# Second cross attention: five of the ten heads that VectorE shifts by their row maximum are shifted on GpSimd

## The reference, cut to what matters

```python
q = layer_norm(query_antecedent @ Wq, gq, bq)
k = layer_norm(key_antecedent @ Wk, gk, bk)
v = layer_norm(value_antecedent @ Wv, gv, bv)
...
sim = jnp.einsum('bhqd,bhkd->bhqk', qh / jnp.sqrt(jnp.float32(dk)), kh)
bias = NEG_BIAS * (~mask).astype(sim.dtype)[:, None]
masked = sim + bias
weights = jax.nn.softmax(masked, axis=-1)
outh = jnp.einsum('bhqk,bhkd->bhqd', weights, vh)
```

## Time and profile before

| what | value |
|---|---|
| median of 3 runs | 1052.25 us |
| lowest and highest of them | 1049.93 and 1054.67 us |
| span of the profiled execution | 1057.6 us |
| busy share of the span: PE, DVE, ACT, POOL | 87%, 74%, 53%, 46% |

### The profile page before, as it was taken

How to read it: one execution, slowest core, us unless ns; L and a number is a source line. 1 busy time by engine, 2 the same in 40 slices (tenths; PEclk the granted TensorE clock), 3 DMA queues, 4 the chain that set the end, 5 groups by cost and what they waited for, 6 DMA issues and landing times.

```text
span 1057.6 us, 19542 instructions
## 1 busy us (share of the span) xinstructions
PE 919.4 (87%) x6337; PEld 655.6 (62%) x6337; DVE 785.7 (74%) x2080; ACT 557.7 (53%) x1494; POOL 490.0 (46%) x451
## 2 busy tenths in 40 slices
PE   6898985888778999869997598988989999989987
PEld 4787533767578989727775243434437677768774
DVE  6889999999756777769998376777734744589982
ACT  4675456886444445724443156766764233445533
POOL 5444553555066564635556777574530600024430
PEclk9999896999879999969999659989999999999998
DMA  9300000000111111410000322222102000000001
GB/s 324 149 1 1 2 6 1 1 1 1 41 39 39 41 40 33 109 66 1 0 1 0 107 67 62 82 76 62 31 1 101 1 1 1 1 2 2 1 1 40
DMA packets 29828, 40.55 MB, mean 38 GB/s; under 512 B 11468, under 2 KB 25036, under 8 KB 29228
## 3 DMA queue, kind: packets, MB, share of 16 engines
q1 hardware_dynamic: 27244, 34.28, 10.3%
q0 software_dynamic: 2496, 5.16, 1.9%
HBM read 31.44 MB, written 7.82 MB: 37 GB/s over the span
## 4 chain that ended last, share of the span: by engine, by line
PE 27%; issue 14%; POOL 7%; DVE 5%; ACT 3%; SPq 1%; DMA 0%; DVEq 0%; POOLq 0%; ACTq 0%
POOL att L1787 6%; PE ps L1163 4%; PE ps L829 4%; PE ps L1135 4%; PE ps L819 4%; PE ps L1147 3%; PE ps L793 1%; PE ps L1249 1%; PE ps L1257 1%; DVE rs L2124 1%; PE ps L1101 1%; DVE stats L2001 0%; SPq L570 0%; PE ps L1106 0%; DVE U L2029 0%
## 5 line engine op out<-in xcount | busy, mean ns | idle before, releaser
L1787 POOL TENSOR_TENSOR att<-att,ri 128x1232 f32<-128x1232 f32 x64 | 169.3, 2645 | 190.5 <-DVE ri L2130 190.5
L793 PE MATMUL ps<-VW,PT 128*128 128x128 f32 (+3 forms) x1280 | 157.6, 278 | 17.5 <-DVE x L2145 16.0
L793 PEld LDWEIGHTS ps<-VW,PT 128*128 128x128 f32 (+1 forms) x1280 | 148.4, 192 | 35.2 <-DVE x L2145 28.3
L1369 ACT ACTIVATE PT<-ps 128x512 f32<-128x512 f32 x128 | 70.6, 594 | 89.5 <-PE ps L766 88.7
L766 PE MATMUL ps<-W,att 128*128 128x128 f32 (+1 forms) x640 | 86.9, 282 | 16.2 <-POOL att L1787 14.7
L1761 POOL TENSOR_TENSOR rstd<-ve,minus_half 128x4 f32<-128x4 f32 x38 | 38.8, 1039 | 114.2 <-DVE ve L2016 97.7
L900 PE MATMUL ps<-PT,att 128*128 128x128 f32 x624 | 80.8, 285 | 8.5 <-issue 8.4
L829 PEld LDWEIGHTS ps<-U,att 128*128 128x128 f32 x512 | 66.3, 191 | 33.1 <-issue 29.1
L766 PEld LDWEIGHTS ps<-W,att 128*128 128x128 f32 (+1 forms) x640 | 72.7, 143 | 22.3 <-POOL att L1787 15.5
L2581 DVE CUSTOM_DVE_ANT_0 C<-ps,cmaskb 128x512 bf16<-128x512 f32 (+1 forms) x128 | 71.1, 555 | 20.7 <-PE ps L1135 18.0
L2581 DVE CUSTOM_DVE_ANT_0 U<-ps,cmaskb 128x384 bf16<-128x384 f32 (+1 forms) x128 | 53.9, 421 | 41.8 <-PE ps L1135 41.5
(11 more groups left out here) (432 smaller groups left out, 2105.6 us busy)
## 6 DMA issues: line engine op xcount, KB each, us to landing
U<-in_ffn SPq DMA_DIRECT2D x1, 6176.0 KB, 23.2
U<-split SPq DMA_DIRECT2D x144, 32.0 KB
W<-split SPq DMA_DIRECT2D x144, 32.0 KB
W<-in_packed SPq DMA_DIRECT2D x1, 2162.5 KB, 23.5
U<-in_ffn SPq DMA_DIRECT2D x1, 2060.0 KB, 9.7
U<-in_moe SPq DMA_DIRECT2D x1, 2048.0 KB, 7.3
split<-VBD SPq DMA_DIRECT2D x4, 384.0 KB, 2.9
split<-W SPq DMA_DIRECT2D x4, 384.0 KB, 2.7
```

The lines of the kernel that those rows point to most:

```text
L793: q = mm(attended(s, t), PT[0:m, t.slot(2), c, :], batch(VW, t.group)[0:m, c * D:(c + 1) * D], start=(c == 0), stop=(c == NC - 1))
L1369: go(PT[:, t.slot(2), 4 * k:4 * k + 4, :].rearrange("p c n -> p (c n)"), ps[:, k0 + k, :], ACT.Copy).then_inc(probsT, 1)
L1787: tt(p, p, over_keys(ri[:, t.slot(2), :]), ALU.mult).then_inc(probs, 1)
```

## The change

`BY_POOL = 5` heads of the ten leave VectorE's shift. GpSimd gets a step `shift(t)` that waits for `rowmax` and adds `mx` to heads 0 to 4 in place, and signals a new semaphore `pool_shifted`; VectorE's `shift` keeps heads 5 to 9. ScalarE's exponential of the ten heads waits for both semaphores. GpSimd's loop for X1 becomes `shift(i)`, `normalize(i-1)`.

The chip's semaphores are limited in number, so that four that VectorE alone used one after the other (`e0_chain`, `m_rec`, `rope_chain`, `sel_chain`) become one, `vector_chain`, with the count at which each user starts (`OUT_CHAIN`, `ROPE_CHAIN`, `SELECT_CHAIN`). Each of those waits stands where it stood.

```diff
+BY_POOL = 5
...
+OUT_CHAIN = (E - HALF - 1) * NT
+ROPE_CHAIN = OUT_CHAIN + UNITS
+SELECT_CHAIN = ROPE_CHAIN + 2 * B
...
+        pool_shifted = sem("pool_shifted")
...
         def over_part(a):
-            return a.unsqueeze(2).to_broadcast([P, SPLIT, KEYS])
+            return a.unsqueeze(2).to_broadcast([P, a.shape[1], KEYS])
...
                         act.wait_ge(shifted, t.n + n0 + 2)
+                        act.wait_ge(pool_shifted, t.n + 1)
                         go(att[:, 2 + t.slot(2), 0:SPLIT * KEYS], att[:, t.slot(2), 0:SPLIT * KEYS], ACT.Exp)\
                             .then_inc(expd, 1)
...
+                def shift(t):
+
+                    pool.wait_ge(rowmax, t.n + n0 + 1)
+                    a = heads(att[:, t.slot(2), :])[:, 0:BY_POOL, :]
+                    tt(a, a, over_part(mx[:, t.slot(2), 0:BY_POOL]), ALU.add).then_inc(pool_shifted, 1)
+                if s == X1:
+                    skewed_loop(pool, [(shift, 0), (normalize, 1)], NT, TB)
+                    return
                 skewed_loop(pool, [(normalize, 0)], NT, TB)
...
                     if s == X1:
-                        tt(a[:, 0:SPLIT, :], a[:, 0:SPLIT, :], over_part(mx[:, t.slot(2), 0:SPLIT]), ALU.add).then_inc(shifted, 1)
+                        tt(a[:, BY_POOL:SPLIT, :], a[:, BY_POOL:SPLIT, :], over_part(mx[:, t.slot(2), BY_POOL:SPLIT]), ALU.add)\
+                            .then_inc(shifted, 1)
```

More of the change, by code:

```diff
@@ L373, in build @@
         side_ps, side_sb, offset_set = sem("side_ps"), sem("side_sb"), sem("offset_set")
-        rot_ps, rope_chain, roped = sem("rot_ps"), sem("rope_chain"), sem("roped")
+        rot_ps, roped = sem("rot_ps"), sem("roped")
         y_set, tables_set, scratch = sem("y_set"), sem("tables_set"), sem("scratch")
         kv_ps, kv_sb, kv_chain = sem("kv_ps"), sem("kv_sb"), sem("kv_chain")
+        pool_shifted = sem("pool_shifted")
         kbd, vbd, vw_ps, vw_sb, vw_bo = map(sem, ("kbd_done", "vbd_done", "vw_ps", "vw_sb", "vw_bo"))
@@ L385, in build @@
         qk_ps, qk_max, kq_ps, kq_exp = map(sem, ("qk_ps", "qk_max", "kq_ps", "kq_exp"))
-        diag_set, pv_ps, oT_sb, m_rec = map(sem, ("diag_set", "pv_ps", "oT_sb", "m_rec"))
+        diag_set, pv_ps, oT_sb = map(sem, ("diag_set", "pv_ps", "oT_sb"))
         first_ps, k_flat, q_flat, k_chain, q_chain, k_split, q_split = map(
@@ L391, in build @@
         stacked = [sem(f"stacked{r}") for r in range(HOLD)]
-        e0_ps, e0_scaled, e0_added, e0_pair, e0_half, e0_chain = map(
-            sem, ("e0_ps", "e0_scaled", "e0_added", "e0_pair", "e0_half", "e0_chain"))
+        e0_ps, e0_scaled, e0_added, e0_pair, e0_half = map(
+            sem, ("e0_ps", "e0_scaled", "e0_added", "e0_pair", "e0_half"))
+        vector_chain = sem("vector_chain")
         up_ps, silu, gated, down_ps = map(sem, ("up_ps", "silu", "gated", "down_ps"))
-        pol, pol_sb, sel_done, sel_chain = sem("pol"), sem("pol_sb"), sem("sel_done"), sem("sel_chain")
+        pol, pol_sb, sel_done = sem("pol"), sem("pol_sb"), sem("sel_done")
         h3_ps, h3_sb, r3_ps, r3_sb, o3_ps = map(sem, ("h3_ps", "h3_sb", "r3_ps", "r3_sb", "o3_ps"))
@@ L2485, in add_scaled @@
                 tt(x[:, t, :], x[:, t, :], hsum[:, t % 2, :], ALU.add).then_inc(x_new, 1)
-            c = Chain(dve, e0_chain)
+            c = Chain(dve, vector_chain)
             for t in range(NT + 1):
@@ L2589, in beside @@
                         .rearrange("p i g (m d) -> p i g m d", m=2)
-                    v.reciprocal(rec[:, :, :, :].unsqueeze(4), o[:, :, :, :, HD:VE]).then_inc(m_rec, 1)
-                    dve.wait_ge(m_rec, n + 1)
+                    v.reciprocal(rec[:, :, :, :].unsqueeze(4), o[:, :, :, :, HD:VE]).then_inc(vector_chain, 1)
+                    dve.wait_ge(vector_chain, OUT_CHAIN + n + 1)
                     half = o_s[:, b * TB:(b + 1) * TB, c * (D // 2):(c + 1) * (D // 2)]
@@ L2633, in _ @@
             mix_and_moments(B - 1)
-            roping = Chain(dve, rope_chain)
+            roping = Chain(dve, vector_chain, ROPE_CHAIN)
             def rope3(b):
@@ L2660, in _ @@
             dve.wait_ge(pol, 2)
-            c = Chain(dve, sel_chain)
+            c = Chain(dve, vector_chain, SELECT_CHAIN)
             lg = ps[:, 7, 0:B * E].rearrange("p (b e) -> p b e", e=E)
```

## The result

The changed kernel takes 1045.68 us (median of 7 runs, 1043.24 to 1049.98), the kernel before beside it 1052.32 (7 runs, 1049.93 to 1058.78): a ratio of 0.9944, 95% interval 0.9922 to 0.9966, about 5.9 us. (The two medians lie 6.6 us apart.) Timed a second time on one chip the ratio was 0.9944 again, 0.9917 to 0.9972. The forecast was 1047.0 us, in the range of 1044.8 to 1050.6; the time fell inside it, and the gain by the ratio is a little more than half a per cent. Three single executions of 1482 to 2187 us, in a slow state, are left out of all medians and ratios.

A forecast was written before the change was run, and what follows sets the result against it. VectorE was taken to bound X1, its tile falling from 5.04 to 4.63 us. Saving 0.4 at X1's start and 4.9 over 12 tiles, 5.3 us, took 1052.25 to 1047.0 us; range 1044.8 to 1050.6.

The forecast's parts named there:

- The bound: X1's even part: VectorE, busy without gaps, sets the tile; halving its shift takes 5.04 us to 4.63.
- GpSimd's shift: New 385 wide GpSimd instruction in X1, 0.83 us, placed in idle time before the normalisation, so costing nothing.
- The normalisation: GpSimd's step in X1, held up by VectorE's shift; to fall from 2.84 to 2.43 us.
- The sum: Main case: X1 saves 0.4 + 4.9 = 5.3 us, giving 1047.0 us; chance 0.68.
- Start of X1: Fourth mask addition, waiting for scores behind the first normalisation, comes 0.4 us sooner.
- The twelve tiles: X1 after the fourth mask addition: 12 tiles each save 0.41 us, 4.92 in all.
- the chain through the scores: Update, product, scores, mask addition to a following update in X1: two tiles in 9.15 to 9.37 us, 4.58 to 4.69 each.
- The closing chain: Rival in X1: a chain of waits through other engines binds before VectorE; 3.5 us saved, 1048.7 us; chance 0.20.
- The port: Rival in X1: GpSimd's shift, beyond about 1.1 us, holds VectorE's shift up; 1060 us at 2.0; chance 0.05 for slower.
- the cast: GpSimd instruction at X2's start in the kernel before; VectorE's shift there took 2.02 us instead of 1.40, losing 0.62.
- Whoever came first held the other up: Claim on VectorE and GpSimd in the same SBUF tile: the earlier instruction delays the later; VectorE once lost 0.62 us.
- The saving did arrive: Answers the rival that later stages give X1's gain back through TensorE's clock, about 1051.5 us; chance 0.07, shared with port.

The follow-up runs named there:

- the loop written out: Changed kernel with VectorE's X1 loop written out for all 16 tiles; 1045.66 us, ratio 0.9938 against the kernel before.
- VectorE's half alone: Changed kernel without GpSimd's shift and ScalarE's second wait, VectorE's shift still 385 wide, heads 0 to 4 unshifted; 1047.5 us, ratio 0.9953.
- the other order: Changed kernel with GpSimd's normalisation of the tile before placed ahead of its shift; 1058.43 us, ratio 1.0049 against the kernel before.
- the run with two GpSimd instructions: Changed kernel where GpSimd adds its shift, then subtracts it in a second equal instruction before signalling; 1049.09 us, ratio 0.9975.

## Why the prediction was right

**The bound.** VectorE set the tile; half of its shift gone made the tile shorter by 0.40 where 0.41 was said (5.04 to 4.64, the loop written out).

**GpSimd's shift.** 0.83 us forecast, 0.827 measured, starting 0.08 after the maximum where 0.09 was said, in the idle time of GpSimd. That it costs nothing there, VectorE's half alone bears out: the same tile without it. That it would cost much elsewhere, the other order showed: 5.50 us a tile, where 5.55 had been worked out before that run.

**The normalisation.** 2.43 forecast, 2.44 measured.

**The sum.** Start of X1: 0.4 us forecast; from first to fourth mask addition it was 15.14 us before (172.26 to 187.40 in the first profile) and 14.74 after (173.38 to 188.12), so 0.40. The twelve tiles: 4.92 forecast, and the fourth to the last addition went from 60.45 (187.40 to 247.85) to 55.91 (188.12 to 244.03), so 4.54. Of the 0.38 missing 0.2 are the two loop heads; the prediction had the chain through the scores there, with its lag of 0.28 and its 4.69, and took it for no bound. The rest is 0.39 to 0.40 a tile where 0.41 was said. The end brought 0.06. Together 5.0 where 5.3 was said. The second pair of profiles gives the same three differences within 0.01 us.

**The rivals.** The closing chain closed at one tile in four, and only by 0.1. The port: GpSimd's shift ends 0.16 us before VectorE's begins, where 0.14 was said. The prediction let it cost from about 1.1 us on, by as much as it lasts longer, so 0.24 us at 1.34; with nine heads on GpSimd VectorE lost 0.275 of the 0.32 us that its shift was shorter (176 ns instead of 496). In the last tile of the run with two GpSimd instructions VectorE lost 0.62 of the 0.72 us that the running instruction still had, as it had lost 0.62 of 0.73 to the cast. "Whoever came first held the other up" needs a margin, as the lead of 0.08 us shows. What I had not priced is the late normalisation, which took about half of X1's gain in that run (88.4 us, against 85.8 and 86.0 in the changed kernel and 90.8 and 91.0 before).

The saving did arrive as far as the medians tell, with a ratio of 0.9944 twice. Single profiles can't show what the stages behind X1 do: from the last update of X1 to the end they took 782.6 to 789.0 us in eleven of the twelve profiles, in no order of the gain, and 794.6 in the first of the kernel before.

**What did not come as said.** The last update was to come some 5.3 us sooner; it came 3.9 to 4.0 sooner, because X1 began later. The change alone need not bring that delay: with the semaphores joined and nothing else X1 began at 171.8 us, with ten heads on GpSimd at 172.2, the kernel before at 172.0 and 172.3, and these four had a granted clock of 0.96 in the first 40 us. Of the eight profiles in which X1 began at 173.0 us or later seven had 0.91 there. Why both profiles of the changed kernel are among these stays open.

**What stays open.** The ratio's 5.9 us are 0.9 more than X1's 5.0. The intervals, 2.3 to 2.9 us to either side, hold the 5.0, and no run here separates the two. That the forecast of the time lies 1.3 us from the median is thus partly luck, since the sum had 0.3 us too much for X1 and the whole came out lower still. What bears the sum out is X1, part by part.

## What to carry to other kernels

Moving part of a bound engine's work to an idle one pays what the bound engine is spared per turn, as long as the helper starts and ends inside a gap that it already has. Read from the timeline when its input is ready and what stands behind it on its queue, since the same instruction one place later made the tile 0.46 us longer instead of 0.4 shorter. Where VectorE and GpSimd both read two inputs in SBUF, work out which is under way when the other begins: either all of it is moved or the two are kept apart in time. And of chains that come out within 0.1 us of the bound, take the one whose lag stood in a row of the same loop, not the shorter lag of another stage.

## What was not expected of the hardware

GpSimd's instruction that by its record began 0.08 us ahead of VectorE's two-input instruction was held up by it (1.25 us instead of 0.83), while the same instruction 0.11 us ahead held VectorE up (1.12 us instead of 0.50), and so did one that had run for 0.98 us (451 ns instead of 176). An estimate from these rows: GpSimd needs the port some 0.14 us after its record's start. The prediction had this figure from the normalisation of the kernel before, and in the run with two instructions GpSimd lost 0.43 of the 0.58 us that VectorE's shift still had at GpSimd's start, which leaves 0.15. Since a lead of 0.08 us was too short and one of 0.11 enough, VectorE's own need would lie 0.03 to 0.06 us after its record's start, by the same estimate. The one profile of a kernel can differ from another of the same kernel by 7.5 us in a stage that the change doesn't touch: the gathers spread over 113.5 us in one profile of the kernel before and over 106.0 in the next.
